# Folding the query and key weights of a cross-attention into one matrix, at the start of a one-core perceiver block

## The chip, the core and the metric

The kernel runs on one core of one Trainium2 chip. A time is the device time of one execution in microseconds (us). The engines are PE (TensorE, matrix products), ACT (ScalarE), DVE (VectorE), POOL (GpSimd) and SP (SyncE, which here only issues DMA transfers). Each engine executes its own list of instructions in order, and engines wait for each other through semaphores.

## The reference

x has 512 tokens of 512 values, ctx has 8192 tokens of 512 values. The block is a cross-attention from x to ctx with a single head, then a linear attention, then a mixture of experts with a convolution, each on a layer norm of x. Only the start of the first step is touched:

```python
qp = layernorm(x) @ Wq.T + bq
kp = ctx @ Wk.T + bk
vp = ctx @ Wv.T + bv
scores = qp @ kp.T * scale          # 512 queries x 8192 keys
x = x + softmax(scores) @ vp @ Wo.T + bo
```

## The kernel before, in words

**Splitting.** Products that need float32 accuracy are made from halves: a matrix a is cut into a high part in the type fp32r (a cast) and a low part (a minus its high part), and a product of two such matrices is three matmuls, high by high, high by low and low by high (`project`, L1162). So each operand costs one cast (mostly on ACT) and one subtraction (on DVE or POOL) before PE can use it.

**Folding of the keys.** ctx is never projected by Wk. The kernel computes qT = Wq times the normalised x, plus bq, and then qk = Wk.T times qT, so that a score is a product of a raw ctx token with a column of qk. This leaves out the dot product of qp with bk, which is the same for all keys of a query. It is needed only where the running maximum is initialised and shifted, and is computed as `key_bias`: DVE multiplies the queries with bk (`qb`, L831), adds the four parts (L852, L855), and PE sums over the partitions by four products with a column of ones (L1281).

**The start, until the first tile of scores.** SP issues the loads in one queue: x and Wq in eight transfers of 256 KB (L337 to L341), the small columns, Wk as one transfer of 1 MB (L343), the first two pairs of transposed ctx tiles, and others. Meanwhile PE multiplies an identity with itself (`warm`, L1179). For each of the four 128-token tiles of x, DVE computes statistics (`ln_stats`), ACT the square root (`std_of`), DVE the scale (`ln_scale`), ACT the normalised tile (`apply_of`), PE its transpose (`transpose_x`), ACT the high half (`high_xT`), DVE the low half (`low_xT`). ACT makes the high halves of Wq and Wk (L550, L570), POOL their low halves (L395, L397). PE computes qT in 96 matmuls of 256 columns (`q_half`), ACT and DVE split it (L589, L833), and PE computes qk in 96 matmuls of 256 columns (L1210 to L1216), which ACT and DVE split again (L602, L840). After that POOL adds bo to x (L410) and, once the last qk product is done, splits Wv (L417, L419).

**The main loop.** In each step s, PE computes one tile of scores for 128 keys (`scores`, L1217, 12 matmuls of 512 columns), ACT copies it to a ring buffer (`keep`), and DVE folds it into a running maximum (`peak`). A tile of scores may start when the peak of the tile two before it is done, since there are two PSUM banks for them. From step 22 on, PE also multiplies exponentials with ctx. Everything on each engine stands in a fixed order that the program writes out; there is no planner.

Of the kernel before, what the change touches and what calls it, by code (L numbers as in the profile page):

```python
# [11 lines left out]
P = 128  # L12
# [32 lines left out]
WARM = 10  # L45
KEEP_WARM = 4
# [19 lines left out]
def perceiver_block(nc, x, ctx_t, ctx_n, wq_t, wk_in, wv_t, wo_t, wqkv_in, wout_in, pieces, cols_in, rows_in, out):  # L66
    with ExitStack() as stack:
# [54 lines left out]
        qT = parts(112, "qT", [P, C, T])  # L122
        qb = at(164, "qb", [P, C, T])
# [22 lines left out]
        block_max, run_max, shift_q, key_bias, biased_max, inv_den = (stat(n) for n in range(6))  # L146
# [61 lines left out]
        wk_loaded = sem("wk_loaded")  # L208
# [7 lines left out]
        wk_high = sem("wk_high")  # L216
        wk_ready = sem("wk_ready")
        wvo_high = sem("wvo_high")
# [22 lines left out]
        q_psum = sem("q_psum")  # L241
        qTh_ready = sem("qTh_ready")
        qTl_ready = sem("qTl_ready")
        qb_step = sem("qb_step")
# [142 lines left out]
        def _(pool):  # L387
# [24 lines left out]
            pool.wait_ge(qk_psum, 2 * C)  # L412
# [94 lines left out]
        Q_BANKS = ((4, 5, 6, 7), (0, 1, 2, 3))  # L507
# [19 lines left out]
        def _(act):  # L527
# [24 lines left out]

            std_of(0)
            apply_of(0)
            high_wq(0)
# [5 lines left out]
            high_wq(1)  # L561
            apply_of(2)
            std_of(3)
            high_wq(2)
            high_xT(2, XT_BANKS)
            apply_of(3)
            high_wq(3)
            high_xT(3, XT_BANKS)
            act.wait_ge(wk_loaded, 16)
            act.copy(wk[0][:], wk_raw[:]).then_inc(wk_high, 1)  # L570
# [14 lines left out]
            def high_q(n):  # L585

                c, h = n % C, n // C * HALF
                act.wait_ge(q_psum, n + 1)
                act.activation(qT[0][:, c, h:h + HALF], bank[:, Q_BANKS[n // C][c], h:h + HALF], ACT.Identity,  # L589
                               bias=col("bq", c)).then_inc(qTh_ready, 1)  # L590

            act.wait_ge(cols_loaded, 16)
            for n in range(C):
                high_q(n)
            for n in range(C):
                high_q(C + n)
                if n < 2:
                    high_ct(n)
            for n in range(2 * C):
                c, h = n % C, n // C * HALF  # L600
                act.wait_ge(qk_psum, n + 1)
                act.copy(qk[0][:, c, h:h + HALF], bank[:, Q_BANKS[n // C][c], h:h + HALF]).then_inc(qkh_ready, 1)  # L602

# [165 lines left out]
        def _(dve):  # L769
# [34 lines left out]

            first_stats(0)
# [10 lines left out]
            low_xT(3, XT_BANKS)  # L816

# [9 lines left out]
            def low_q(n):  # L827
                c, h = n % C, n // C * HALF
                dve.wait_ge(qTh_ready, n + 1)

                dve.tensor_scalar(qb[:, c, h:h + HALF], bank[:, Q_BANKS[n // C][c], h:h + HALF], col("bq", c),  # L831
                                  col("bk", c), ALU.add, ALU.mult).then_inc(qb_step, 1)
                dve.scalar_tensor_tensor(out=qT[1][:, c, h:h + HALF], in0=bank[:, Q_BANKS[n // C][c], h:h + HALF],  # L833
                                         scalar=col("bq", c), in1=qT[0][:, c, h:h + HALF].bitcast(F32), op0=ALU.add,
                                         op1=ALU.subtract).then_inc(qTl_ready, 1)

            def low_qk(n):
                c, h = n % C, n // C * HALF
                dve.wait_ge(qkh_ready, n + 1)
                dve.tensor_tensor(qk[1][:, c, h:h + HALF], bank[:, Q_BANKS[n // C][c], h:h + HALF],  # L840
                                  qk[0][:, c, h:h + HALF].bitcast(F32), ALU.subtract).then_inc(qkl_ready, 1)

            for n in range(C):
                low_q(n)
            for n in range(C):
                low_q(C + n)
                if n < 2:
                    low_ct(n)
            low_qk(0)

            dve.wait_ge(qb_step, 2 * C)
            dve.tensor_tensor(qb[:, 0:2, :], qb[:, 0:2, :], qb[:, 2:4, :], ALU.add).then_inc(qb_step, 1)  # L852
            low_qk(1)
            dve.wait_ge(qb_step, 2 * C + 1)
            dve.tensor_tensor(qb[:, 0, :], qb[:, 0, :], qb[:, 1, :], ALU.add).then_inc(qb_step, 1)  # L855
            for n in range(2, 2 * C):
                low_qk(n)
            dve.wait_ge(keyb_psum, 1)
            dve.tensor_copy(key_bias[:], bank[:, MISC, 0:TT]).then_inc(init_done, 1)
            dve.memset(run_max[:], LOWEST).then_inc(init_done, 1)  # L860
            dve.wait_ge(init_done, 2)
# [18 lines left out]
            def new_shift(n):  # L880

                dve.wait_ge(top_psum, n + 1)
                dve.reduce_max(block_max[:], bank[:, MISC, :].rearrange("p (t k) -> p t k", t=TT),
# [53 lines left out]
            for s in range(TILES + AHEAD - 1):  # L937
# [15 lines left out]
                if s < TILES:  # L953
                    peak(s)

# [199 lines left out]
        def _(pe):  # L1155
# [33 lines left out]
            def q_half(h, e):  # L1189

                pe.wait_ge(xl_ready, 2 * (h + 1))
                pe.wait_ge(wq_ready, e + 1)
                part = slice(h * HALF, (h + 1) * HALF)
                project(Q_BANKS[h][e], [cut(wq, e, c * P, (c + 1) * P) for c in range(C)],
                        [cut(xT, c, part.start, part.stop) for c in range(C)], cols=part).then_inc(q_psum, 1)

            transpose_x(0)
            warm(KEEP_WARM)
            transpose_x(1)
            warm(KEEP_WARM)  # L1200
            q_half(0, 0)
            transpose_x(2)
            q_half(0, 1)
            transpose_x(3)
            q_half(0, 2)
            q_half(0, 3)
            for e in range(C):
# [354 lines left out]
```

## Time and profile before

| what | us |
|---|---|
| median of 3 runs | 556.14 (556.11 to 556.38) |
| the profiled execution's own time | 555.92 |
| its span, first to last instruction | 553.9 |
| PE busy | 542.2 (98%) |
| DVE busy | 350.3 (63%) |
| ACT busy | 257.0 (46%) |
| POOL busy | 201.6 (36%) |

All times of day below are microseconds from the start of the span. A row of the timeline begins with the start and the duration; "x8" says that so many instructions of one kind were merged into the row, with the time from the first start to the last end. A matmul's duration includes the pipeline behind it, so what one costs in a stream is the distance from one start to the next. The square bracket at the end of a row is the idle time before it, with the instruction that ended it.

### The profile page before, as it was taken

What the parts mean: (1) busy time and instruction counts of PE and PEld (TensorE: products, weight loads), DVE (VectorE), ACT (ScalarE), POOL (GpSimd) and SP (SyncE); (2) the same over time, 40 slices, a digit from 0 to 9 for tenths busy, and PEclk for the clock granted to TensorE, in tenths of its full rate; (3) what the DMA queues carried; (4) which work ended last, traced back from release to release, by engine and by line L of the source; (5) the groups of instructions that cost most, each with busy time, mean ns of one, the idle gap of its engine ahead of it and who ended that gap; (6) DMA issues with size and microseconds to landing.
All of it is one profiled execution on the core that took longest, in us unless ns stands there. A gap on an engine that the chain in (4) does not pass through costs nothing. (4 is left out here: it accounts for less than half of the span.)

```text
span 553.9 us, 7074 instructions
## 1 busy us (share of the span) xinstructions
PE 542.2 (98%) x2616; PEld 453.1 (82%) x2616; DVE 350.3 (63%) x574; ACT 257.0 (46%) x420; POOL 201.6 (36%) x125
## 2 busy tenths in 40 slices
PE   8999999999999999999999999979999999999997
PEld 8998888888888888888888887868787889878886
DVE  5845555764667766567766579959736226628757
ACT  6624336754445545445455346546355442561210
POOL 3860512332113251311145133797058709800000
PEclk9999999999999999999999999999999999999999
DMA  8602522425321242232223123132202203300002
GB/s 332 246 14 78 186 83 111 145 84 178 126 77 76 81 148 77 76 141 88 77 76 115 38 115 114 57 134 99 92 0 72 81 1 115 114 1 1 0 2 76
DMA packets 14002, 51.61 MB, mean 93 GB/s; under 512 B 1680, under 2 KB 1680, under 8 KB 13072
## 3 DMA queue, kind: packets, MB, share of 16 engines
q1 hardware_dynamic: 13968, 51.16, 25.7%
q8 instruction: 21, 0.34, 0.3%
q14 instruction: 13, 0.11, 0.1%
HBM read 50.11 MB, written 1.05 MB: 92 GB/s over the span
## 5 line engine op out<-in xcount | busy, mean ns | idle before, releaser
L450 POOL TENSOR_TENSOR cn_l<-raw_n,cn_h 128x1024 fp32r<-128x1024 f32 x32 | 81.3, 2543 | 203.6 <-ACT cn_h L583 203.6
L1241 PE MATMUL bank<-ph,cn_h 128*128 128x512 f32 x256 | 101.5, 396 | 4.7 <-POOL cn_l L450 3.0
L877 DVE TENSOR_TENSOR top<-top,bank 128x512 f32<-128x512 f32 x60 | 41.2, 687 | 101.5 <-ACT ring L607 101.3
L1242 PE MATMUL bank<-pl,cn_h 128*128 128x512 f32 x256 | 100.4, 392 | 0.0
L1243 PE MATMUL bank<-ph,cn_l 128*128 128x512 f32 x256 | 100.3, 392 | 0.0
L1230 PE MATMUL bank<-qk_h,ct_h 128*128 128x512 f32 x256 | 100.0, 391 | 0.0
L1232 PE MATMUL bank<-qk_h,ct_l 128*128 128x512 f32 x256 | 99.7, 389 | 0.0
L1231 PE MATMUL bank<-qk_l,ct_h 128*128 128x512 f32 x256 | 99.6, 389 | 0.0
L613 ACT ACTIVATE ph<-ring 128x512 fp32r<-128x512 f32 x64 | 40.4, 632 | 76.2 <-PE bank L1243 45.2
L607 ACT COPY ring<-bank 128x512 f32<-128x512 f32 x64 | 37.6, 587 | 81.7 <-PE bank L1232 81.7
L1241 PEld LDWEIGHTS bank<-ph,cn_h 128*128 128x128 f32 x256 | 48.4, 189 | 16.0 <-POOL cn_l L450 3.4
L904 DVE TENSOR_TENSOR ring<-ring,shift_b 128x512 f32<-128x512 f32 x64 | 59.4, 928 | 0.0
L1243 PEld LDWEIGHTS bank<-ph,cn_l 128*128 128x128 f32 x256 | 48.5, 189 | 10.4
L1242 PEld LDWEIGHTS bank<-pl,cn_h 128*128 128x128 f32 x256 | 48.5, 189 | 9.8
L1232 PEld LDWEIGHTS bank<-qk_h,ct_l 128*128 128x128 f32 x256 | 48.1, 188 | 10.1
L1230 PEld LDWEIGHTS bank<-qk_h,ct_h 128*128 128x128 f32 x256 | 48.0, 188 | 10.1 <-issue 0.3
L1231 PEld LDWEIGHTS bank<-qk_l,ct_h 128*128 128x128 f32 x256 | 48.1, 188 | 9.8
L912 DVE TENSOR_TENSOR pl<-bank,ph 128x512 fp32r<-128x512 f32 x64 | 43.7, 682 | 7.2 <-ACT bank L618 7.1
L618 ACT ACTIVATE bank<-ring 128x512 f32<-128x512 f32 x64 | 37.6, 588 | 11.1 <-DVE psum_keys L926 10.3
L926 DVE TENSOR_TENSOR psum_keys<-psum_keys,bank 128x512 f32<-128x512 f32 x63 | 42.6, 676 | 0.1
L821 DVE TENSOR_TENSOR ct_l<-raw_t,ct_h 128x1024 fp32r<-128x1024 f32 x32 | 41.0, 1282 | 2.4 <-ACT ct_h L575 2.4
L575 ACT CAST ct_h<-raw_t 128x1024 fp32r<-128x1024 f32 x32 | 33.7, 1052 | 0.0
(214 smaller groups left out, 911.1 us busy)
## 6 DMA issues: line engine op xcount, KB each, us to landing
raw_t<-ctx_t SPq DMA_DIRECT2D x32, 512.0 KB, 4.1
raw_n<-ctx_n SPq DMA_DIRECT2D x32, 512.0 KB, 3.3
piece_raw<-pieces SPq DMA_DIRECT2D x12, 512.0 KB, 3.3
w_raw<-wqkv_in SPq DMA_DIRECT2D x3, 1024.0 KB, 4.9
xs<-x SPq DMA_DIRECT2D x4, 256.0 KB, 3.4
wq_raw<-wq_t SPq DMA_DIRECT2D x4, 256.0 KB, 4.1
wk_raw<-wk_in SPq DMA_DIRECT2D x1, 1024.0 KB, 6.4
wvo_raw<-wv_t SPq DMA_DIRECT2D x1, 1024.0 KB, 11.5
```

The source lines that it names most:

```text
L450: pool.tensor_tensor(cn[p % CNB][1][:], raw_n[p % 2][:], cn[p % CNB][0][:].bitcast(F32), ALU.subtract).then_inc(cnl_ready, 1)
L821: dve.tensor_tensor(ct[p % 2][1][:], raw_t[p % 2][:], ct[p % 2][0][:].bitcast(F32), ALU.subtract).then_inc(ctl_ready, 1)
L877: dve.tensor_tensor(top[n % 2][:], top[n % 2][:], bank[:, S_BANKS[i % 2], :], ALU.max).then_inc(max_done, 1)
L904: dve.tensor_tensor(ring[:, q % RING, :], ring[:, q % RING, :], shift_b[q // SB % 2][:], ALU.subtract).then_inc(sub_done, 1)
L912: dve.tensor_tensor(pl[q % PB][:], bank[:, p_bank(q), :], ph[q % PB][:].bitcast(F32), ALU.subtract).then_inc(pl_ready, 1)
L926: dve.tensor_tensor(psum_keys[:], psum_keys[:], bank[:, p_bank(q), :], ALU.add).then_inc(den_done, 1)
L1230: pe.matmul(bank[:, dst, :], ct[i // 2 % 2][0][:, c, keys], qk[0][:, c, :], start=(c == 0), stop=False)
L1231: pe.matmul(bank[:, dst, :], ct[i // 2 % 2][0][:, c, keys], qk[1][:, c, :], start=False, stop=False)
L1232: ins = pe.matmul(bank[:, dst, :], ct[i // 2 % 2][1][:, c, keys], qk[0][:, c, :], start=False, stop=(c == C - 1))
L1241: pe.matmul(bank[:, c, :], keys[0][:, q % 2, d], ph[q % PB][:], start=first, stop=False)
L1242: pe.matmul(bank[:, c, :], keys[0][:, q % 2, d], pl[q % PB][:], start=False, stop=False)
L1243: return pe.matmul(bank[:, c, :], keys[1][:, q % 2, d], ph[q % PB][:], start=False, stop=final)
```

## The change

Wq and Wk are multiplied with each other first. The new matrix `wqk` = Wq.T Wk (512 by 512) is computed from the weights alone, by 48 matmuls of 512 columns in four steps e, each of which needs one 128-row piece of each weight, and the transposes of the x tiles are placed between them (`transposed_at`). ACT casts it, DVE subtracts (the low half), and PE computes qk = wqk.T times the normalised x in 48 matmuls of 512 columns. The two biases now come in separately: Wk.T bq is added to qk (`qk_bias`), and the bias of a query is the dot product of its normalised x with Wq.T bk, plus the dot product of bq with bk.

```diff
-WARM = 10
-KEEP_WARM = 4
+WARM = 16
@@ SP
-            for t in range(0, TT, 2):
-                for n in range(t, t + 2):
-                    sp.dma_start(xs[:, n, :], x[n]).then_inc(x_loaded[n], 16)
-                for e in range(t, t + 2):
-                    sp.dma_start(wq_raw[:, e, :], wq_t[e]).then_inc(wq_loaded[e], 16)
+            for e in range(C):
+                sp.dma_start(wq_raw[:, e, :], wq_in[e]).then_inc(wq_loaded[e], 16)
+                sp.dma_start(wk_raw[:, e, :], wk_in[e]).then_inc(wk_loaded[e], 16)
+                sp.dma_start(xs[:, e, :], x[e]).then_inc(x_loaded[e], 16)
             sp.dma_start(cols[:], cols_in).then_inc(cols_loaded, 16)
-            sp.dma_start(wk_raw[:], wk_in).then_inc(wk_loaded, 16)
@@ POOL
-            for e in range(C):
-                pool.wait_ge(wq_high, e + 1)
-                pool.tensor_tensor(wq[1][:, e, :], wq_raw[:, e, :], wq[0][:, e, :].bitcast(F32), ALU.subtract).then_inc(wq_ready, 1)
-            pool.wait_ge(wk_high, 1)
-            pool.tensor_tensor(wk[1][:], wk_raw[:], wk[0][:].bitcast(F32), ALU.subtract).then_inc(wk_ready, 1)
+            pool.memset(ones[:], 1.0).then_inc(ones_ready, 1)
+            for e in range(1, C):
+                pool.wait_ge(wk_loaded[e], 16)
+                pool.tensor_copy(wk[0][:, e, :], wk_raw[:, e, :]).then_inc(wk_high, 1)
+                pool.wait_ge(wk_high, e)
+                pool.tensor_tensor(wk[1][:, e, :], wk_raw[:, e, :], wk[0][:, e, :].bitcast(F32), ALU.subtract).then_inc(wk_ready, 1)
...
-            pool.wait_ge(qk_psum, 2 * C)
+            pool.wait_ge(wqk_psum, C)
@@ ACT
+            high_wq(0)
+            act.wait_ge(wk_loaded[0], 16)
+            act.copy(wk[0][:, 0, :], wk_raw[:, 0, :]).then_inc(wk0_high, 1)
             std_of(0)
+            high_wq(1)
             apply_of(0)
             std_of(1)
+            high_wq(2)
             apply_of(1)
             high_xT(0, XT_BANKS)
             std_of(2)
+            high_wq(3)
+            apply_of(2)
             high_xT(1, XT_BANKS)
             std_of(3)
+            apply_of(3)
             high_xT(2, XT_BANKS)
             high_xT(3, XT_BANKS)
+            for c in range(C):
+                act.wait_ge(wqk_psum, c + 1)
+                act.copy(wqk[0][:, c, :], bank[:, WQK_BANKS[c], :]).then_inc(wqkh_ready, 1)
+            for n in range(2):
+                high_ct(n)
+            act.wait_ge(qk_bias_ready, 1)
+            act.wait_ge(bk_step, C)
+            for c in range(C):
+                act.wait_ge(qk_psum, c + 1)
+                act.activation(qk[0][:, c, :], bank[:, QK_BANKS[c], :], ACT.Identity, bias=qk_bias[:, c:c + 1]).then_inc(qkh_ready, 1)
@@ DVE
+            def low_wq(e):
+                dve.wait_ge(wq_high, e + 1)
+                dve.tensor_tensor(wq[1][:, e, :], wq_raw[:, e, :], wq[0][:, e, :].bitcast(F32), ALU.subtract).then_inc(wq_ready, 1)
+            low_wq(0)
+            dve.tensor_tensor(wk[1][:, 0, :], wk_raw[:, 0, :], wk[0][:, 0, :].bitcast(F32), ALU.subtract).then_inc(wk0_ready, 1)
             first_stats(0)
             ln_scale(0)
+            low_wq(1)
             first_stats(1)
             ln_scale(1)
+            low_wq(2)
             first_stats(2)
             low_xT(0, XT_BANKS)
             ln_scale(2)
+            low_wq(3)
             low_xT(1, XT_BANKS)
             first_stats(3)
             ln_scale(3)
             low_xT(2, XT_BANKS)
             low_xT(3, XT_BANKS)
+            for c in range(C):
+                dve.tensor_tensor(wqk[1][:, c, :], bank[:, WQK_BANKS[c], :], wqk[0][:, c, :].bitcast(F32),
+                                  ALU.subtract).then_inc(wqkl_ready, 1)
-            for n in range(C):
-                low_q(n)
-            for n in range(C):
-                low_q(C + n)
-                if n < 2:
-                    low_ct(n)
-            low_qk(0)
...
+            def weigh_rows(dst, raw, loaded, name, step):
+                for e in range(C):
+                    dve.wait_ge(loaded[e], 16)
+                    if e == 0:
+                        ins = dve.tensor_scalar(dst[:], raw[:, e, :], col(name, e), None, ALU.mult)
+                    else:
+                        dve.wait_ge(step, e)
+                        ins = dve.scalar_tensor_tensor(out=dst[:], in0=raw[:, e, :], scalar=col(name, e), in1=dst[:],
+                                                       op0=ALU.mult, op1=ALU.add)
+                    ins.then_inc(step, 1)
+            weigh_rows(bq_wk, wk_raw, wk_loaded, "bq", bq_step)
+            weigh_rows(bk_wq, wq_raw, wq_loaded, "bk", bk_step)
+            dve.tensor_tensor(b_prod[:], cols[:, a:a + C], cols[:, b:b + C], ALU.mult).then_inc(dot_step, 1)
+            dve.wait_ge(dot_step, 1)
+            dve.reduce_sum(b_dot[:, 0:1], b_prod[:], AX.X).then_inc(dot_step, 1)
+            dve.memset(run_max[:], LOWEST).then_inc(run_cleared, 1)
+            for n in range(2):
+                low_ct(n)
+            dve.wait_ge(qk_bias_psum, 1)
+            dve.tensor_copy(qk_bias[:], bank[:, MISC, 0:C]).then_inc(qk_bias_ready, 1)
+            for c in range(C):
+                dve.wait_ge(qkh_ready, c + 1)
+                dve.scalar_tensor_tensor(out=qk[1][:, c, :], in0=bank[:, QK_BANKS[c], :], scalar=qk_bias[:, c:c + 1],
+                                         in1=qk[0][:, c, :].bitcast(F32), op0=ALU.add, op1=ALU.subtract).then_inc(qkl_ready, 1)
+            def key_term(t):
+                dve.tensor_tensor(key_terms[:, t, :], xn[:, t, :], bank[:, U_BANK, :], ALU.mult).then_inc(key_step, 1)
+                dve.wait_ge(key_step, 2 * t + 1)
+                dve.reduce_sum(key_bias[:, t:t + 1], key_terms[:, t, :], AX.X).then_inc(key_step, 1)
...
                 if s < TILES:
                     peak(s)
+                if 2 <= s < 2 + TT:
+                    key_term(s - 2)
@@ PE
+            transposed_at = {(1, 1): 0, (2, 0): 1, (2, 3): 2, (3, 1): 3}
+            for e in range(C):
+                pe.wait_ge(wq_ready, e + 1)
+                if e == 0:
+                    pe.wait_ge(wk0_ready, 1)
+                else:
+                    pe.wait_ge(wk_ready, e)
+                for c in range(C):
+                    fold_part(e, c)
+                    if (e, c) in transposed_at:
+                        transpose_x(transposed_at[e, c])
+            pe.wait_ge(xl_ready, TT)
+            for e in range(C):
+                pe.wait_ge(wqkl_ready, e + 1)
+                if e == C - 1:
+                    pe.wait_ge(bq_step, C)
+                    for c in range(C):
+                        ins = pe.matmul(bank[:, MISC, c:c + 1], bq_wk[:, c * P:(c + 1) * P], ones[:], start=True, stop=True)
+                    ins.then_inc(qk_bias_psum, 1)
+                for c in range(C):
+                    ins = project(QK_BANKS[c], [cut(wqk, e, c * P, (c + 1) * P)], [cut(xT, e, 0, T)], starts=(e == 0),
+                                  stops=(e == C - 1))
@@ PE, after the first tile of scores
-                    for n in range(TT):
-                        ins = pe.matmul(bank[:, MISC, n:n + 1], qb[:, 0, n * P:(n + 1) * P], ones[:], start=True, stop=True)
+                    pe.matmul(bank[:, U_BANK, :], ones[:].to_broadcast([P, P]), bk_wq[:], start=True, stop=True)
+                    pe.matmul(bank[:, MISC, C:C + 1], ones[:].to_broadcast([P, P]), b_dot[:, 0:1], start=True, stop=True)
```

In the diff, `low_wq(e)` makes the low half of one piece of Wq, and `fold_part(e, c)` is a `project` of 3 matmuls of 512 columns. The tiles `qk` lie where `wq_raw` and `wk_raw` lie, so that ACT's first write of `qk` waits for both chains of `weigh_rows`. `scores(0)` waits for the first piece of the low half of qk, as before.

## Rows read from the trace of the kernel before

**Rows 1.** The page, busy time of each engine.
```profile
PE 542.2 (98%) x2616; PEld 453.1 (82%) x2616; DVE 350.3 (63%) x574; ACT 257.0 (46%) x420; POOL 201.6 (36%) x125
```

**Rows 2.** Timeline of PE, from its first product to the second tile of scores.
```profile
1.52 4.64 PE L1181 MATMUL bank<-ident 128*128 128x128 f32 x20 [1.52 <-POOL ident L390]
...
7.00 1.09 PE L1181 MATMUL bank<-ident 128*128 128x128 f32 x8
...
10.12 0.39 PE L1169 MATMUL bank<-xT_h,wq_h 128*128 128x256 f32 x1 [0.56 <-DVE xT_l L797]
...
22.89 0.28 PE L1169 MATMUL bank<-qT_h,wk_h 128*128 128x256 f32 x1
...
34.41 0.40 PE L1230 MATMUL bank<-qk_h,ct_h 128*128 128x512 f32 x1
...
37.16 0.95 PE L1281 MATMUL bank<-ones,qb 128*128 128x1 f32 x8
37.97 0.49 PE L1230 MATMUL bank<-qk_h,ct_h 128*128 128x512 f32 x1
```

**Rows 3.** The loads of Wq (issue line, then landing) and of Wk.
```profile
L341 SPq DMA_DIRECT2D wq_raw<-wq_t x4: 424/432/432, 1.6 to 4.0; - x4
...
DMA to landing us min/median/max: 3.6/4.1/4.6
...
wk_raw<-wk_in SPq DMA_DIRECT2D x1, 1024.0 KB, 6.4
```

**Rows 4.** Timeline of ACT and of DVE over the first x tile.
```profile
5.22 0.81 ACT L545 ACTIVATE xn<-xs,shift,rstd 128x512 f32<-128x512 f32 x1 [0.48 <-DVE shift L790]
5.95 0.60 ACT L550 CAST wq_h<-wq_raw 128x512 fp32r<-128x512 f32 x1
...
3.41 0.69 DVE L781 BATCH_NORM_STATS2 stats<-xs 128x6 f32<-128x512 f32 x1 [3.41 <-DMA xs<-x]
...
4.98 0.21 DVE L790 TENSOR_SCALAR shift<-mv,rstd 128x1 f32<-128x1 f32 x1
...
8.45 0.69 DVE L797 TENSOR_TENSOR xT_l<-bank,xT_h 128x512 fp32r<-128x512 f32 x1 [0.35 <-ACT xT_h L538]
```

**Rows 5.** Groups by line: the first ns min/median/max, the others busy us, mean ns.
```profile
L821 DVE TENSOR_TENSOR ct_l<-raw_t,ct_h x32: 1210/1218/2343, 21.4 to 305.6; 128x1024 fp32r<-128x1024 f32 x32
...
L1137 DVE SCALAR_TENSOR_TENSOR conv<-xf,cols,conv 128x512 f32<-128x512 f32 x12 | 9.0, 752 | 0.4
L667 ACT ACTIVATE vT_h<-bank,cols 128x512 fp32r<-128x512 f32 x4 | 2.7, 689 | 3.4 <-PE bank L1169 3.4
L1135 DVE TENSOR_SCALAR conv<-xf,cols 128x512 f32<-128x512 f32 x4 | 2.2, 542 | 0.0
```

**Rows 6.** Timeline of POOL: the additions of bo, and a cast of Wv.
```profile
23.02 7.04 POOL L410 TENSOR_TENSOR xs<-xs,rows 128x512 f32<-128x512 f32 x4
34.64 1.04 POOL L417 CAST wv_h<-wvo_raw 128x1024 fp32r<-128x1024 f32 x1 [4.58 <-PE bank L1169]
```

**Rows 7.** Timeline of DVE beside POOL, at 29 us and at 354 us.
```profile
29.15 1.45 DVE L855 TENSOR_TENSOR qb<-qb 128x512 f32<-128x512 f32 x1
...
354.04 1.70 DVE L904 TENSOR_TENSOR ring<-ring,shift_b 128x512 f32<-128x512 f32 x1
...
352.33 2.86 POOL L445 TENSOR_TENSOR w_k_l<-w_raw,w_k_h 128x1024 fp32r<-128x1024 f32 x1
355.14 2.86 POOL L450 TENSOR_TENSOR cn_l<-raw_n,cn_h 128x1024 fp32r<-128x1024 f32 x1
```

**Rows 8.** PE after an idle time, then a window; 0.57 is its granted clock.
```profile
370.80 0.50 PE L1241 MATMUL bank<-ph,cn_h 128*128 128x512 f32 x1 [2.98 <-POOL cn_l L450]
...
373.56 0.63 PE L1241 MATMUL bank<-ph,cn_h 128*128 128x512 f32 x1
373.98 0.63 PE L1242 MATMUL bank<-pl,cn_h 128*128 128x512 f32 x1
...
372.00:374.00 2.00, 2.00 (x7) 1.55 (x7) 0.00 (x0) 1.06 (x2) 1.09 (x1) 0.57 0.71 289
```

More of the change, by code:

```diff
@@ L63, with perceiver_block @@
 NROWS = 3 * D + E
-def perceiver_block(nc, x, ctx_t, ctx_n, wq_t, wk_in, wv_t, wo_t, wqkv_in, wout_in, pieces, cols_in, rows_in, out):
+def perceiver_block(nc, x, ctx_t, ctx_n, wq_in, wk_in, wv_t, wo_t, wqkv_in, wout_in, pieces, cols_in, rows_in, out):
     with ExitStack() as stack:
@@ L121, in perceiver_block @@
         wk_raw = at(152, "wk_raw", [P, C, D])
-        qT = parts(112, "qT", [P, C, T])
-        qb = at(164, "qb", [P, C, T])
+        wqk = parts(112, "wqk", [P, C, D])
+        bk_wq = at(164, "bk_wq", [P, D])
+        bq_wk = at(166, "bq_wk", [P, D])
+        key_terms = at(100, "key_terms", [P, TT, D])
         wvo_raw = at(176, "wvo_raw", [P, C, D])
@@ L144, in stat @@
             return small[:, n * TT:(n + width) * TT]
-        block_max, run_max, shift_q, key_bias, biased_max, inv_den = (stat(n) for n in range(6))
+        block_max, run_max, shift_q, key_bias, biased_max, inv_den, b_prod, b_dot, qk_bias = (stat(n) for n in range(9))
         kvmask = at(172.5, "kvmask", [P, VW])
@@ L207, in perceiver_block @@
         wq_loaded = [sem(f"wq_loaded{e}") for e in range(C)]
-        wk_loaded = sem("wk_loaded")
+        wk_loaded = [sem(f"wk_loaded{e}") for e in range(C)]
         wv_loaded = sem("wv_loaded")
@@ L240, in perceiver_block @@
         xf_ready = sem("xf_ready")
[L241 to L244, printed above, removed]
+        wqk_psum = sem("wqk_psum")
+        wqkh_ready = sem("wqkh_ready")
+        wqkl_ready = sem("wqkl_ready")
+        bq_step = sem("bq_step")
+        bk_step = sem("bk_step")
+        dot_step = sem("dot_step")
+        qk_bias_psum = sem("qk_bias_psum")
+        qk_bias_ready = sem("qk_bias_ready")
+        key_step = sem("key_step")
+        run_cleared = sem("run_cleared")
         wr_high = sem("wr_high")
@@ L825, in _ @@
             dve.wait_ge(cols_loaded, 16)
[L827 to L835, printed above, removed]
@@ L849, in _ @@
-            low_qk(0)
[L851 to L859, printed above, removed]
@@ new lines, in key_term @@
+            def key_term(t):
+                dve.wait_ge(keyb_psum, 1)
+                dve.tensor_tensor(key_terms[:, t, :], xn[:, t, :], bank[:, U_BANK, :], ALU.mult).then_inc(key_step, 1)
+                dve.wait_ge(key_step, 2 * t + 1)
+                dve.reduce_sum(key_bias[:, t:t + 1], key_terms[:, t, :], AX.X).then_inc(key_step, 1)
+                if t == TT - 1:
+                    dve.wait_ge(key_step, 2 * TT)
+                    dve.tensor_tensor(key_bias[:], key_bias[:], bank[:, MISC, C:C + 1].to_broadcast([P, TT]),
+                                      ALU.add).then_inc(init_done, 1)
@@ L882, in new_shift @@
                 dve.wait_ge(top_psum, n + 1)
+                if n == 0:
+                    dve.wait_ge(run_cleared, 1)
+                    dve.wait_ge(init_done, 1)
                 dve.reduce_max(block_max[:], bank[:, MISC, :].rearrange("p (t k) -> p t k", t=TT),
@@ L1187, in transpose_x @@
                 transpose_tile(xn, t, XT_BANKS[t]).then_inc(xnT_psum, 1)
-            def q_half(h, e):
-                pe.wait_ge(xl_ready, 2 * (h + 1))
-                pe.wait_ge(wq_ready, e + 1)
[L1193 to L1206, printed above, removed]
-            for e in range(C):
-                q_half(1, e)
-            pe.wait_ge(wk_ready, 1)
-            for h in range(2):
-                pe.wait_ge(qTl_ready, (h + 1) * C)
-                part = slice(h * HALF, (h + 1) * HALF)
+            def fold_part(e, c):
+                d = slice(c * P, (c + 1) * P)
+                ins = project(WQK_BANKS[c], [cut(wq, e, d.start, d.stop)], [cut(wk, e, 0, D)], starts=(e == 0),
+                              stops=(e == C - 1))
+                if e == C - 1:
+                    ins.then_inc(wqk_psum, 1)
@@ L1214, in _ @@
+            for e in range(C):
+                pe.wait_ge(wqkl_ready, e + 1)
+                if e == C - 1:
+                    pe.wait_ge(bq_step, C)
+                    pe.wait_ge(ones_ready, 1)
+                    for c in range(C):
+                        ins = pe.matmul(bank[:, MISC, c:c + 1], bq_wk[:, c * P:(c + 1) * P], ones[:], start=True, stop=True)
+                    ins.then_inc(qk_bias_psum, 1)
                 for c in range(C):
-                    project(Q_BANKS[h][c], [cut(wk, e, c * P, (c + 1) * P) for e in range(C)],
-                            [cut(qT, e, part.start, part.stop) for e in range(C)], cols=part).then_inc(qk_psum, 1)
+                    ins = project(QK_BANKS[c], [cut(wqk, e, c * P, (c + 1) * P)], [cut(xT, e, 0, T)], starts=(e == 0),
+                                  stops=(e == C - 1))
+                    if e == C - 1:
+                        ins.then_inc(qk_psum, 1)
```

58 lines of the change are left out of this document (18 added, 40 removed).

## The prediction, made before the changed kernel had run

> **What bounds the kernel now.** I read the busy times first: PE is busy for 98% of the span [rows 1], so over nearly all of it only PE's work counts. The timeline of PE at the start comes second [rows 2]: the first product with Wq starts at 10.12, the first tile of scores at 34.41, and between them stand 192 matmuls of 256 columns. The 96 of the second product run from 22.89 to 34.41 without a gap, 0.120 us from start to start. The 12 matmuls of 512 columns of a tile of scores go from 34.41 to 37.16, 0.229 us each. After the start nothing of the change touches PE's stream but one small product, so the question is at what time the first tile of scores begins. The third view was the timelines of ACT, DVE and POOL over the first 40 us [rows 4 to 7], because a chain through those three feeds PE there, and the profile's 98% says nothing of how near to it they come.
>
> **PE's own work.** Removed: 192 x 0.120 = 23.0 us. Added: 96 x 0.229 = 22.0. That is a gain of 1.0. The four products with a column of ones (8 instructions, 37.16 to 37.97, 0.81 [rows 2]) now stand inside the second product, as `qk_bias`, and cost 0.8 there. After the first tile of scores come instead one unsplit 128x512 product and one of a single column. A 128-column instruction of that kind takes 1.09/8, about 0.11 with its tail taken off [rows 2], so 512 columns take 2 x 0.44, and the column 0.2: 1.1 for 0.8, a loss of 0.3 (bounds 0 and 1.0).
>
> The Trainium skill has a rule that disputes the gain: TensorE: Matmul & The Clock Gate, section "Back-to-back issue gap", puts an isolated gap at N/2.4 + 2.5 ns. By it an estimate of the saving is 192 x 0.109 less 96 x 0.216, some 0.2 us and not 1.0; the rows' 0.120 and 0.229 differ from it, and they decide.
>
> **Where the first product starts.** Eight loads of 256 KB land from 3.41 (the first, which DVE waited for [rows 4]) to 4.0 + 4.6 = 8.6 [rows 3], 0.74 apart; Wk's megabyte lands at 11.4, the same rate. In the new order that gives Wq's first piece 3.4, Wk's 4.1, x 4.9, and so on to the last x at 11.4. ACT casts (0.60), DVE subtracts (0.69): piece 0 of both is ready at 5.5. But PE first does 16 warm products, 32 instructions. The 20 of before took 4.64 from 1.52, 0.21 each, and from 7.00 on they took half of that: TensorE went from 1.2 to 2.4 GHz at 7.0, after products since 1.52 [rows 2]. So 26 run at the slow rate and 6 at 0.11: the first product starts at 7.7 (5.5 and 8.3 are the bounds; it matters little, as the next paragraph shows).
>
> **The chain through the x tiles.** ACT's `high_xT(0)` now stands ahead of the work on tile 2, and the transpose of tile 0 stands behind 18 matmuls: 7.7 + 18 x 0.229 + 4 x 0.11 = 12.3. Then cast 0.6, `low_xT(0)` 0.7, `ln_scale(2)` 0.4, `apply_of(2)` 0.8 [rows 4]: 14.8. `high_xT(1)`, `low_xT(1)`: 16.1. Statistics to shift of tile 3 take 1.78 (3.41 to 5.19), `apply_of(3)` 0.8: 18.7. PE is ready to transpose tile 3 then as well. Casts of tiles 2 and 3: 20.0, last low half 20.8. ACT casts wqk from 20.0, DVE subtracts its four pieces at 0.6 apart: 21.4 to 23.2. PE has finished wqk at about 20.7, idles 0.8, and starts the second product at 21.5. Without a further wait it ends at 21.5 + 48 x 0.229 + 0.8 = 33.3, 1.1 before the 34.41 of now. PE's 0.8 of idle takes back most of what the products save.
>
> **DVE's queue behind it, which decides.** From 23.2 DVE has, in order: eight operations of `weigh_rows`, three small ones, `low_ct` twice, and only then the copy of `qk_bias`, for which ACT waits before it may write qk, and through it `scores(0)`. Prices: `tensor_scalar` 0.54, `scalar_tensor_tensor` 0.75, in a chain on one tile 0.79 each; `low_ct` 1.22 [rows 5], a small one 0.2, as the shift [rows 4]. Alone that is 2 x (0.55 + 3 x 0.79) + 0.5 + 2.4 = 8.7: the copy ends at 31.8, ACT's 0.69 and DVE's 0.75 give 33.4, and PE would hardly wait.
>
> But POOL works at the same time. Its four additions of bo wait for the last x tile and run from 18.8 to 24.0 (1.3 each alone, 7.04 together beside DVE [rows 6]); its split of Wv, formerly released by the last product at 34.6, is now released at 20.7 and follows at once. The rows show what this does. DVE's addition at 29.15, both inputs in SBUF, took 1.45 for the usual 0.7: it ended 0.55 after POOL's addition did at 30.06 [rows 6, 7]. At 354 it is a pattern: DVE's L904 issued at 354.04, ended at 355.74, 0.55 after POOL's subtraction at 355.19; POOL's next, issued at 355.14, ended 2.26 after DVE's [rows 7]. The two run one after the other, each a whole instruction, turn by turn. With these steps (DVE ends 0.62 after POOL, being 0.07 longer; POOL's subtraction 2.26 after DVE, its cast of 1.04 some 0.9 after):
> bq1 24.6, cast 25.5, bq2 26.1, subtraction 28.4, bq3 29.0, cast 29.9, bk0 29.6, bk1 30.5, subtraction 32.8, bk2 33.4, bk3 34.2; the small ones 34.6, `low_ct` to 37.0, copy 37.1, ACT 37.8, DVE 38.6, PE 38.7.
> This takes the two `tensor_scalar` as free of the collision, as no row shows one; if they take part too, the same steps end at 39.7 and the first chain ends at 30.2, so that the last quarter of the second product also waits. I take the middle, 39.2: 4.8 after the 34.41 of now.
>
> That a `scalar_tensor_tensor` collides is not in my rows, only that a `tensor_tensor` with two inputs in SBUF does. On this the Trainium skill, SBUF — State Buffer, section "Who interferes with whom", says that any DVE instruction with two SBUF inputs contends with a GpSimd one that reads SBUF, and that the second to issue blocks for the whole instruction; the rows agree for the additions. It also names `tensor_scalar` among those that can take the shared ports, which by the steps above would be 39.7, and 0.5 more than my sum.
>
> **The clock.** PE then idles for about 5.5 us, from 33.3 on. In the trace of now PE idled for 2.98 before 370.80 and soon after ran 512-column matmuls 0.42 apart at a granted 0.57, the 1.2 GHz level for the most part [rows 8]; eight of them, some 3.4 us of PE, cost 8 x (0.42 - 0.229) = 1.5. At the start the slow rate lasted 5.5 us [rows 2], which would cost 2.7. I take 2.0.
>
> **What stays hidden.** `key_term` adds 0.7 for the product and 0.7 for the sum (the statistics' 0.69 is the nearest row [rows 4]) in four steps. A step has 2.75 of PE; DVE's own work in two is 2 x 0.6 + 1.15, so four steps hold 10.5 of 11. A tile of scores needs the peak of two tiles before, so DVE may be over a microsecond late. Nothing, at worst 2.8. The smaller warm-up groups and the POOL work on Wk lie beside other work: POOL's piece takes 0.55 + 1.3, ready 2 to 3 us before PE comes to it. The missing `init_done` wait of `high_cn(0)` ends nothing late.
>
> **Sum.** 4.8 + 2.0 + 0.3 = 7.1. The profiled execution took 555.92, with 553.9 of span and 2.0 around it; it becomes 563.0. The median of the runs is 0.2 above it: 563.2.
>
> **Rivals.**
> *The queue fits.* POOL and DVE don't collide on these operations, or POOL's turns fall beside ACT's. For it: DVE's work alone ends at 31.8, and all PSUM-fed DVE operations of the trace keep their time beside POOL. Against: rows 7. PE starts scores at 33.3 to 33.4: -1.0 + 0.3, and up to 1 more if the loads or the clock come early, some 554.9 (553.9 to 556.0). This is the other side; it decides if the copy of `qk_bias` ends before 33.0.
> *Only plain `tensor_tensor` collides.* The chains run freely to 28.9, the product of the biases waits for POOL's second subtraction (to 30.9), `low_ct` follows, copy 33.8, PE 35.4: 1.0 + 0.3 slower with an idle time of 2 that leaves the clock, 557.4.
> *key_term isn't hidden.* Its whole 2.8 stalls scores on top of the forecast: 566.0. Against: the slack above.
>
> **Chances.** The forecast 0.58 (its own range 560.7 to 565.0: half a microsecond from the `tensor_scalar`, 0.7 from the clock, 1 from the x chain), the queue fits 0.24, only `tensor_tensor` 0.10, key_term 0.08. What this kernel's measurement can tell from no change is 0.2%, 1.1 us, so the bound of faster is 555.0. Of the first rival 0.16 lies below it and 0.08 above. With the others: faster 0.17, same 0.10, slower 0.73. The range for 8 in 10 must reach down into the first rival: 554.8 to 565.3.
>
> **What would show it.** Right: DVE's `scalar_tensor_tensor` of `weigh_rows` well over 0.75, most of all 2 to 3 beside POOL's subtractions; ACT's qk activation released by DVE's `qk_bias`; PE idle by 4 to 6 before L1230's successor, then 0.43 spacing. The product of 96 matmuls at 0.229 shows the gain of 1.0. Wrong: all eight at 0.55 to 0.8, POOL's Wv split later, or the second product itself starting after 23.

## The result, and the profile after

| | before | after |
|---|---|---|
| median of the runs, us | 556.12 (555.79 to 556.38) | 562.87 (562.49 to 564.09) |
| ratio, 95% interval | 1 | 1.0125 (1.0108 to 1.0143) |
| profiled execution, us | 555.92 | 562.95 |
| its span, us | 553.9 | 561.2 |
| first tile of scores starts | 34.41 | 39.34 |
| mean granted clock of TensorE | 0.996 | 0.991 |

The change makes the kernel 6.8 us slower; 563.2 was predicted. The busy times say almost nothing of it. PE, with 1.8 us more than in [rows 1], now has 96 instructions fewer, and DVE has 11 us more:

```profile
PE 544.0 (97%) x2520; PEld 449.2 (80%) x2520; DVE 361.6 (64%) x580; ACT 255.5 (46%) x413; POOL 197.3 (35%) x126
```

The timeline of PE, against [rows 2], shows all of it (start us, duration us, engine, line, operation, count, and in brackets the idle time before and what ended it):

```profile
1.52 6.26 PE L1206 MATMUL bank<-ident 128*128 128x128 f32 x32 [1.52 <-POOL ident L397]
7.54 0.48 PE L1194 MATMUL bank<-wk_h,wq_h 128*128 128x512 f32 x1
...
21.55 0.47 PE L1194 MATMUL bank<-xT_h,wqk_h 128*128 128x512 f32 x1 [0.70 <-DVE wqk_l L831]
...
30.02 1.02 PE L1241 MATMUL bank<-ones,bq_wk 128*128 128x1 f32 x8
30.90 0.48 PE L1194 MATMUL bank<-xT_h,wqk_h 128*128 128x512 f32 x1
...
33.52 0.39 PE L1194 MATMUL bank<-xT_h,wqk_l 128*128 128x512 f32 x1
39.34 0.77 PE L1262 MATMUL bank<-qk_h,ct_h 128*128 128x512 f32 x1 [5.43 <-DVE qk_l L869]
39.91 0.63 PE L1263 MATMUL bank<-qk_l,ct_h 128*128 128x512 f32 x1
...
44.41 1.02 PE L1312 MATMUL bank<-bk_wq,ones 128*128 128x512 f32 x2
45.26 0.28 PE L1313 MATMUL bank<-small,ones 128*128 128x1 f32 x2
45.40 0.48 PE L1262 MATMUL bank<-qk_h,ct_h 128*128 128x512 f32 x1
```

Three differences against [rows 2] are to be read here. The scores start at 39.34 for 34.41: 4.93 later. Their first tile lasts from 39.34 to 44.41, 5.07 for 2.75: 2.32 more. What stands behind it lasts from 44.41 to 45.40, 0.99 for 0.81: 0.18 more. Together that is 7.43, and the spans differ by 7.3, so all that comes after the start of the second tile of scores takes back only 0.1.

The windows of the same trace (window, its length, busy us and count of PE, PEld, DVE, ACT and POOL, granted clock, DMA share, GB/s) give the second difference its reason. The granted clock falls while PE is idle (1.00 between 34 and 36, 0.84 between 36 and 38), then stands at 0.50, the 1.2 GHz level, until close to 44:

```profile
36.00:38.00 2.00, 0.00 (x0) 0.00 (x0) 1.62 (x3) 0.34 (x1) 0.00 (x0) 0.84 0.23 63
38.00:40.00 2.00, 0.66 (x2) 0.59 (x3) 1.55 (x3) 2.00 (x4) 0.00 (x0) 0.50 0.91 272
...
44.00:46.00 2.00, 2.00 (x9) 1.30 (x9) 0.69 (x1) 0.59 (x1) 0.00 (x0) 0.96 0.00 0
```

What PE waits for is the end of DVE's queue, which is seen in DVE's timeline:

```profile
23.11 1.11 DVE L848 TENSOR_SCALAR bq_wk<-wk_raw,cols 128x512 f32<-128x512 f32 x1
24.33 5.58 DVE L851 SCALAR_TENSOR_TENSOR bq_wk<-wk_raw,cols,bq_wk 128x512 f32<-128x512 f32 x3
29.84 2.60 DVE L848 TENSOR_SCALAR bk_wq<-wq_raw,cols 128x512 f32<-128x512 f32 x1
32.54 2.47 DVE L851 SCALAR_TENSOR_TENSOR bk_wq<-wq_raw,cols,bk_wq 128x512 f32<-128x512 f32 x3
...
37.47 0.15 DVE L865 COPY small<-bank 128x4 f32<-128x4 f32 x1
38.45 2.73 DVE L869 SCALAR_TENSOR_TENSOR qk_l<-bank,small,qk_h 128x512 fp32r<-128x512 f32 x4 [0.83 <-ACT qk_h L604]
```

The two groups of L851 are the same operation three times, 5.58 us against 2.47. One line's instructions, with their ns (least, median, most), show that they are not uniformly slow:

```profile
L851 DVE SCALAR_TENSOR_TENSOR bq_wk<-wk_raw,cols,bq_wk x3: 1337/1342/2696, 24.3 to 28.6; 128x512 f32<-128x512 f32 x3
L851 DVE SCALAR_TENSOR_TENSOR bk_wq<-wq_raw,cols,bk_wq x3: 751/753/753, 32.5 to 34.3; 128x512 f32<-128x512 f32 x3
```

The last three, at 0.75, start just after POOL has ended its fourth instruction, at 32.16. POOL's timeline of that stretch:

```profile
18.90 5.05 POOL L417 TENSOR_TENSOR xs<-xs,rows 128x512 f32<-128x512 f32 x4 [3.88 <-ACT xn L554]
23.89 1.24 POOL L424 CAST wv_h<-wvo_raw 128x1024 fp32r<-128x1024 f32 x1
25.21 2.71 POOL L426 TENSOR_TENSOR wv_l<-wvo_raw,wv_h 128x1024 fp32r<-128x1024 f32 x1
27.87 1.50 POOL L424 CAST wv_h<-wvo_raw 128x1024 fp32r<-128x1024 f32 x1
29.45 2.71 POOL L426 TENSOR_TENSOR wv_l<-wvo_raw,wv_h 128x1024 fp32r<-128x1024 f32 x1
```

Lay the two beside each other. DVE's three `scalar_tensor_tensor` of `bq` end at 25.67, 28.47 and 29.91, its `bk` 0 at 32.44; POOL's end at 25.13, 27.92, 29.37 and 32.16. Each of DVE's ends 0.54 or 0.55 (the `tensor_scalar` 0.28) after one of POOL's. This looks like turns, each a whole instruction; the experiments test it. And ACT's qk activation was released by DVE's copy:

```profile
37.66 2.42 ACT L604 ACTIVATE qk_h<-bank,small 128x512 fp32r<-128x512 f32 x4 [13.73 <-DVE small L865]
```

`key_term`, the last part, is hidden. Its product (0.68) and sum (0.69) stand in the timeline of DVE four times from 52.41 on, and ACT's copies of the tiles of scores stay 2.72 apart beside them.

### The profile page after: what moved, and what is told of

It reads as the page before. It is cut to its first block and busy times, and to the rows that moved or that the text cites. A ratio compares the mean times of both kernels' runs of the same rounds, so it can differ in the third digit from the quotient of the medians.

```text
span 561.2 us, 6888 instructions
## 1 busy us (share of the span) xinstructions
PE 544.0 (97%) x2520; PEld 449.2 (80%) x2520; DVE 361.6 (64%) x580; ACT 255.5 (46%) x413; POOL 197.3 (35%) x126
## 5 line engine op out<-in xcount | busy, mean ns | idle before, releaser
L837 DVE TENSOR_TENSOR ct_l<-raw_t,ct_h 128x1024 fp32r<-128x1024 f32 x32 | 39.7, 1243 | 1.8 <-ACT ct_h L588 1.8
```

## The experiments

The theory: DVE's queue ahead of the copy of `qk_bias` is late because each of its operations with two inputs in SBUF takes turns with one of POOL's, and the idle time that this makes on PE costs the clock as well. The rivals: DVE's queue is simply too long, or its operations chained on one tile are slow by themselves; or DVE and POOL share bandwidth, each slowed evenly, and take no turns; or the second product, the loads or `key_term` are late. The first four kernels ran beside the kernel before at 556.03 (555.63 to 556.82), the other four beside it at 555.97 (555.73 to 557.04).

**1. `e1_late_split`: POOL's split of Wv waits for the last product, as before the change.**

```diff
-            pool.wait_ge(wqk_psum, C)
+            pool.wait_ge(qk_psum, C)
```

> POOL's split of Wv waits for the last product of qk again instead of the last product of wqk; all else as changed. Turn-taking theory (DVE and POOL instructions that read SBUF twice exclude each other, a whole instruction at a time): only the additions of bo, until 24.0, stand against DVE's chains. bq chain ends at 26.7, bk chain at 29.6, the copy of qk_bias at 32.5, scores begin at 34.2 (39.34 with the change), PE idles by under 1 us and keeps its clock: 555.8 us, range 555.2 to 556.8. Rival, the chained DVE operations are slow by themselves (in-place, one waiting for the other): no change, 562.9. Rival, POOL and DVE share bandwidth evenly: the operations fall from 1.85 to 0.75 too, so this run does not part it from the first.

Measured: 555.73 (554.84 to 556.48), ratio 0.9992 (0.9983 to 1.0002). One wait on another engine gives all of the loss back. What is left of the fold is 0.3 us, which is not clear of the noise. DVE's timeline, then POOL's, then PE's:

```profile
24.33 2.46 DVE L851 SCALAR_TENSOR_TENSOR bq_wk<-wk_raw,cols,bq_wk 128x512 f32<-128x512 f32 x3
26.71 0.48 DVE L848 TENSOR_SCALAR bk_wq<-wq_raw,cols 128x512 f32<-128x512 f32 x1
...
32.22 0.15 DVE L865 COPY small<-bank 128x4 f32<-128x4 f32 x1
```

```profile
33.73 1.04 POOL L424 CAST wv_h<-wvo_raw 128x1024 fp32r<-128x1024 f32 x1 [9.79 <-PE bank L1194]
34.85 2.40 POOL L426 TENSOR_TENSOR wv_l<-wvo_raw,wv_h 128x1024 fp32r<-128x1024 f32 x1
```

```profile
34.09 0.47 PE L1262 MATMUL bank<-qk_h,ct_h 128*128 128x512 f32 x1 [0.43 <-DVE qk_l L869]
```

The same queue with the same instructions is 5.25 us earlier at the copy, and the scores start 5.25 earlier. So the queue is not too long by itself, its operations are not slow by themselves (L851 takes 2.46 for three in both groups), and the second product, the loads and `key_term` are not the cause. Even sharing of bandwidth would give the same result here; the third and fourth kernels part it from the turns. A `tensor_scalar` alone takes 0.48; beside POOL's subtraction it took 2.60. POOL's subtraction at 34.85 runs for its first microsecond beside DVE's operations that read one input from PSUM (until 35.93), and takes the usual 2.4.

**2. `e2_keep_busy`: PE multiplies the identity with itself during the idle time; DVE and POOL unchanged.**

```diff
+            for n in range(24):
+                pe.matmul(bank[:, U_BANK, 0:P], ident[:], ident[:], start=True, stop=True)
             def scores(i):
```

> The changed kernel with 24 extra products of the identity (48 instructions, 5.3 us at 0.11) on PE between the last qk product and the first tile of scores, in a bank that nothing else uses then. Theory that the idle time costs twice, as waiting and as a lower clock behind it: scores still begin at 39.3 to 39.5, but their matmuls stand 0.23 apart and not 0.43, 2.3 us less: 560.6 us (560.2 to 561.0). Rival, the clock falls whatever PE does there or the small products don't hold it: 562.9.

Measured: 560.83 (560.44 to 561.14), ratio 1.0083 (1.0068 to 1.0098).

```profile
34.06 5.52 PE L1250 MATMUL bank<-ident 128*128 128x128 f32 x48
39.63 0.47 PE L1265 MATMUL bank<-qk_h,ct_h 128*128 128x512 f32 x1
```

The scores start no earlier, but their first tile is 2.81 long (39.63 to 42.44) and not 5.07, at a granted clock of 1.00. So the clock's share of the loss is 2.0 us by the medians and 2.3 by the traces, and it follows from PE's idle time.

**3. `e3_small_turns`: Wv and Wo split in pieces of 256 columns, the same work in four times as many instructions.**

```diff
-                    pool.tensor_copy(w[0][:, part, :], ...)
-                    pool.tensor_tensor(w[1][:, part, :], ...)
                     ...
+                    for k in range(4):
+                        c, a = 2 * h + k // 2, k % 2 * 256
+                        pool.tensor_copy(w[0][:, c, a:a + 256], ...)
+                        pool.tensor_tensor(w[1][:, c, a:a + 256], ...)
```

> The changed kernel with POOL's split of Wv and Wo cut into pieces of 256 columns, eight casts and eight subtractions per weight in place of two and two. Turn-taking theory: a DVE operation waits for at most one small POOL instruction (0.3 or 0.65), so a scalar_tensor_tensor beside the split takes 1.0 to 1.4 and none over 1.7; but POOL goes on until 37, so low_ct is met as well: copy of qk_bias at 36, scores at 37.9, 561.3 us (560.3 to 562.3). Rival, even sharing of bandwidth: the operations keep their mean of 1.85 and the time stays at 562.9 or above.

Measured: 559.30 (558.78 to 559.76), ratio 1.0056 (1.0041 to 1.0071). The direction was right, the size was missed by 2.0, outside the stated range. DVE's line, two rows of POOL, and PE's first matmul of scores:

```profile
L852 DVE SCALAR_TENSOR_TENSOR bq_wk<-wk_raw,cols,bq_wk x3: 750/751/1037, 23.7 to 25.7; 128x512 f32<-128x512 f32 x3
```

```profile
23.97 1.11 POOL L427 TENSOR_TENSOR wv_l<-wvo_raw,wv_h 128x256 fp32r<-128x256 f32 x1
25.03 0.85 POOL L425 CAST wv_h<-wvo_raw 128x256 fp32r<-128x256 f32 x1
```

```profile
35.70 0.75 PE L1263 MATMUL bank<-qk_h,ct_h 128*128 128x512 f32 x1 [2.63 <-DVE qk_l L870]
```

I had expected every operation of DVE to wait for a turn, 1.0 to 1.4 each; four of the six took 0.75. The ones that did began 0.14 or 0.15 before the end of a cast (25.73 beside the one that ends at 25.88), and so had next to nothing to wait for. Only the middle one of each chain, issued at 24.59 beside a subtraction that ends at 25.08, took 1.04, and ended 0.55 after it. POOL waited as well: its subtraction took 1.11 here and 0.73 later, beside no such operation of DVE. An operation of DVE thus pays what is left of POOL's instruction when its turn comes, and short instructions leave little. Evenly shared bandwidth does not fit operations of 0.75 and 1.04 beside the same work. After 2.63 us of idle the clock fell again (0.50 between 36 and 38), and the first tile of scores took 4.42 (35.70 to 40.12), 1.6 more than in the second kernel.

**4. `e4_big_turns`: the opposite, one cast and one subtraction of 2048 columns.**

```diff
-                for h in range(2):
-                    pool.tensor_copy(w[0][:, part, :], ...)
-                    pool.tensor_tensor(w[1][:, part, :], ...)
                 ...
+                pool.tensor_copy(w[0][:], wvo_raw[:])
+                pool.tensor_tensor(w[1][:], wvo_raw[:], w[0][:].bitcast(F32), ALU.subtract)
```

> The opposite of the small turns: the split of a weight in one cast (2.0 us) and one subtraction (4.65 us) of 2048 columns. Turn-taking theory: one scalar_tensor_tensor of the bq chain takes some 2.5 and one 5.2 us, the others after them 0.75, since POOL is done by then. The bq chain ends at 32.7 instead of 29.9, so PE's last quarter of qk waits nearly 3 us; the copy of qk_bias at 38.5, scores at 40.2: 563.3 us (562.3 to 564.3). Rival, even sharing: all operations slowed alike, to 1.5 to 2, none at 5, and the time as with the change, 562.9.

Measured: 563.14 (562.61 to 563.84), ratio 1.0129 (1.0112 to 1.0146). DVE's line, POOL's timeline and PE's:

```profile
L848 DVE SCALAR_TENSOR_TENSOR bq_wk<-wk_raw,cols,bq_wk x3: 750/2191/4887, 23.8 to 31.1; 128x512 f32<-128x512 f32 x3
```

```profile
23.31 2.11 POOL L422 CAST wv_h<-wvo_raw 128x2048 fp32r<-128x2048 f32 x1
25.50 4.90 POOL L424 TENSOR_TENSOR wv_l<-wvo_raw,wv_h 128x2048 fp32r<-128x2048 f32 x1
```

```profile
31.91 1.04 PE L1238 MATMUL bank<-ones,bq_wk 128*128 128x1 f32 x8 [2.50 <-issue]
...
39.11 0.47 PE L1259 MATMUL bank<-qk_h,ct_h 128*128 128x512 f32 x1 [1.72 <-DVE qk_l L866]
```

One of DVE's operations of 0.75 took 4.89, the length of POOL's subtraction, one took 2.19, and the third 0.75: turns, and no even sharing. Two operations lose 5.6 us where four lost 5.2 in the changed kernel, and the scores start at 39.11. Part of the clock's loss moves: it falls after PE's 2.50 of idle ahead of the biases' product, is paid in the last quarter of the second product (0.43 between matmuls from 33.39 on), and is back before the scores, which 1.72 us of idle do not slow.

The total, however, was expected rightly by luck. The first tile of scores now takes 2.82 and ends at 41.93, 2.5 before the changed kernel's 44.41, yet the spans differ by only 0.3. Some 2.0 are lost again at 75 us, where POOL splits Wo, also in one piece. POOL's row, DVE's and PE's:

```profile
68.61 4.61 POOL L424 TENSOR_TENSOR wo_l<-wvo_raw,wo_h 128x2048 fp32r<-128x2048 f32 x1
```

```profile
69.29 5.00 DVE L834 TENSOR_TENSOR ct_l<-raw_t,ct_h 128x1024 fp32r<-128x1024 f32 x1 [0.27 <-ACT ct_h L585]
```

```profile
75.04 0.47 PE L1259 MATMUL bank<-qk_h,ct_h 128*128 128x512 f32 x1 [1.92 <-DVE top L894]
```

DVE's subtraction, which takes 1.2 alone, is held for 5.00 behind POOL's; the running maximum comes after it in DVE's queue, and PE waits for that. It is the same cause at a second place, and it was not in my expectation.

**5. `e5_in_gaps`: three of the eight operations of `weigh_rows` put where DVE is idle between x tiles, the other five behind wqk, with `bq` and `bk` alternating so that each is ready when the one before it ends; POOL early as in the change.** The question was whether POOL only gets its turn in a gap of DVE's.

```diff
             first_stats(2)
+            dve.wait_ge(cols_loaded, 16)
+            weigh(0, "bq")
             low_xT(0, XT_BANKS)
             ln_scale(2)
             low_wq(3)
+            weigh(0, "bk")
             ...
+            weigh(1, "bq")
             low_xT(2, XT_BANKS)
             ...
-            weigh_rows(bq_wk, wk_raw, wk_loaded, "bq", bq_step)
-            weigh_rows(bk_wq, wq_raw, wq_loaded, "bk", bk_step)
+            weigh(1, "bk")
+            weigh(2, "bq")
+            weigh(2, "bk")
+            weigh(3, "bq")
+            weigh(3, "bk")
```

> POOL as in the changed kernel (Wv split early), but three of the eight operations of the two bias chains stand in idle stretches of DVE before the second product, and the other five follow it with bq and bk in turn, so that no operation waits for the one just before it. If the ports change hands at the end of every instruction for which the other engine waits: the five end at 33.3, copy of qk_bias 36.1, scores 37.8, the clock lost as before, 561.3 us (560.5 to 562). If POOL only got its turns in the small gap in which DVE waited for its own last result: DVE runs through, copy at 30 to 31, scores at 33.5, about 555.2.

Measured: 560.69 (558.89 to 562.08), ratio 1.0079 (1.0056 to 1.0101). The turns change after every instruction, also where DVE's next is ready at once. DVE's timeline, and PE's:

```profile
24.14 1.52 DVE L819 SCALAR_TENSOR_TENSOR bq_wk<-wk_raw,cols,bq_wk 128x512 f32<-128x512 f32 x1
25.58 2.88 DVE L819 SCALAR_TENSOR_TENSOR bk_wq<-wq_raw,cols,bk_wq 128x512 f32<-128x512 f32 x1
```

```profile
37.02 0.47 PE L1281 MATMUL bank<-qk_h,ct_h 128*128 128x512 f32 x1 [3.14 <-DVE qk_l L888]
```

Beside a cast DVE's operation takes 1.52, beside a subtraction 2.88, and each ends 0.55 after POOL's. In this profiled execution, the fastest of its four at 558.89, PE's first tile of scores took 2.82 (37.02 to 39.84) after 3.14 us of idle: no slow stretch. Where the spread of its times, 3.2 us, comes from is open. A clock that fell in the other three could explain part of it (it cost 1.6 to 2.3 in the kernels above), but those three lie 2.1 apart at one and the same mean granted clock, 0.994, and only the fastest has a trace.

**6. `e6_gaps_late`: the fifth with the wait of the first.** DVE's queue is then shorter and free of POOL.

```diff
  (as e5_in_gaps, and)
-            pool.wait_ge(wqk_psum, C)
+            pool.wait_ge(qk_psum, C)
```

> The same order of DVE, and POOL's split of Wv late again. Both theories: bias chains done by 27, low_ct by 30, copy of qk_bias right after its product at 30.8; scores follow the last qk product at 33.5 without a wait (34.09 with the late split alone): 555.1 us (554.6 to 555.6). Rival, the operations put into the gaps delay the x chain by their own length: 555.7 or more.

Measured: 555.13 (554.73 to 555.42), ratio 0.9982 (0.9973 to 0.9991). PE now goes from the second product into the scores without an idle time. They start 0.90 before the 34.41 of the kernel before, and the medians differ by 0.84:

```profile
33.51 0.39 PE L1281 MATMUL bank<-qk_h,ct_h 128*128 128x512 f32 x1
```

**7. `e7_wqk_first`: also aims at PE's 0.7 of idle between the products**, by casting and subtracting the first quarter of wqk ahead of the x tiles 2 and 3.

```diff
  (as e6_gaps_late, and on ACT; on DVE low_wqk likewise)
+            high_wqk(0)
             high_xT(2, XT_BANKS)
             high_xT(3, XT_BANKS)
-            for c in range(C):
+            for c in range(1, C):
                 high_wqk(c)
```

> As the one before, and the first quarter of wqk is cast and subtracted ahead of the transposes of the last two x tiles, on ACT and DVE: PE's idle time between the two products falls from 0.7 to near 0, the second product starts at 20.8 instead of 21.5: 554.4 us (554.0 to 555.0). Rival, the last x tile is then what PE waits for: no change against the one before.

Measured: 554.36 (553.97 to 554.71), ratio 0.9969 (0.9957 to 0.9981). It is faster than both kernels, 8.5 us below the changed one, with the change's products kept. The scores start 0.86 before the sixth's. Of that, 0.36 is the idle time between the products (0.34 left of 0.70, which the last x tile ends, the wait that the rival named), and 0.5 came with the start of this execution, where the clock rose earlier and PE's first product stands at 6.47, not 7.56. How much of the 0.77 between the two medians is the new order is therefore not settled.

```profile
20.68 0.50 PE L1223 MATMUL bank<-xT_h,wqk_h 128*128 128x512 f32 x1 [0.34 <-DVE xT_l L804]
...
32.65 0.40 PE L1291 MATMUL bank<-qk_h,ct_h 128*128 128x512 f32 x1
```

**8. `e8_warm12`: the seventh with four warm products fewer**, since the first wqk product waited for them and not for the loads.

```diff
-WARM = 16
+WARM = 12
```

> As the one before with 12 warm products in place of 16: the first product starts at 6.7 instead of 7.5, its first matmuls at the slower clock; the transpose of tile 0, which holds ACT's queue, comes 0.7 earlier: 553.8 us (553.3 to 554.4). Rival, the weights' second pieces (ready at 9.6) or the loads of x take over: 554.4 as before.

Measured: 555.54 (553.98 to 556.52, eleven times), ratio 0.9984 (0.9974 to 0.9994): 1.2 slower than the seventh where 0.6 faster was expected. In its trace PE's first product is earlier, 6.09 for 6.47, but at 10 us the engines meet in another order. DVE and POOL of the seventh, then of the eighth:

```profile
10.06 0.69 DVE L814 TENSOR_TENSOR wq_l<-wq_raw,wq_h 128x512 fp32r<-128x512 f32 x1
```

```profile
10.06 1.85 POOL L405 TENSOR_TENSOR wk_l<-wk_raw,wk_h 128x512 fp32r<-128x512 f32 x1
```

```profile
10.06 1.83 DVE L814 TENSOR_TENSOR wq_l<-wq_raw,wq_h 128x512 fp32r<-128x512 f32 x1
```

```profile
10.04 1.29 POOL L405 TENSOR_TENSOR wk_l<-wk_raw,wk_h 128x512 fp32r<-128x512 f32 x1
```

Where both issue at 10.06, DVE takes 0.69 and POOL waits; where POOL is 0.02 us ahead, DVE takes 1.83. That 1.1 us runs down the chain of the x tiles: the last transposes, which PE runs at 18.30 in the seventh, come 1.26 later, and so do the scores (33.92 for 32.65):

```profile
19.56 0.65 PE L1213 MATMUL bank<-ident,xn 128*128 128x128 f32 x4 [1.53 <-ACT xn L554]
```

Whether fewer warm products flip this order, or it falls either way by chance, is not settled. The eleven times lie partly at 554 to 555 and mostly at 555.5 to 556.5, which fits a race that goes both ways, but only one of the eleven has a trace.

## Why the prediction was right

- **PE's own work, -1.0.** Right. 36 matmuls of the second product stand between 21.55 and 29.82, 0.230 each, for the 0.229 predicted.
- **The first product and the x tiles.** 7.54 for 7.7; transposes of tile 0 at 11.75 for 12.3; low halves of wqk up to 23.19 for 23.2; second product at 21.55 for 21.5. It ends at 33.75 and not 33.3, mostly since the biases' product takes 1.08 (29.82 to 30.90, a wait for `bq_wk` in it) and not 0.8. That is hidden in the idle time.
- **DVE's queue beside POOL.** The step that decides, and right: the copy ends at 37.62, predicted 37.1 with the `tensor_scalar` free and about 38 with them colliding. The turns fell otherwise than in my list: `bq` 1 met the first cast, so the first subtraction fell on `bq` 2 and the second on the `tensor_scalar` of `bk`. Both `tensor_scalar` took part, the first held by the last addition of bo (1.11 for 0.48), the second for 2.60. That is the later of my two ends, with the first chain at 30.2 (29.91 measured) and the scores at 39.7 (39.34 measured). I had not decided between the ends and took the middle, 39.2; that it came within 0.14 is luck, as the rule of the later end is the true one and its steps were 0.4 too long. (The 31.8 that I gave for the queue alone is 31.9 by its own terms.)
- The Trainium skill, SBUF — State Buffer, section "Who interferes with whom", names both kinds, an instruction with two SBUF inputs and, as one that can contend, `tensor_scalar`; the trace agrees with both (1.34 and 2.70 for 0.75; 2.60 for 0.48).
- **The clock, 2.0.** Right in kind, 2.32 in the trace. I had sized it from eight slow matmuls at 370 us; it was eleven, the first 0.57 from the next and ten 0.43, up to 44.17.
- **The bias product at the end, 0.3.** It was 0.18: the unsplit 512-column product takes 0.85 (44.41 to 45.26), and the single column 0.14, not 0.2.
- **`key_term`, 0.** Right.
- **The sum.** 4.8 + 2.0 + 0.3 = 7.1; measured 4.93 + 2.32 + 0.18 = 7.43. Between the profiled executions there are 7.03, as 0.1 came back after the second tile and the time around the span was 1.75 here and not 2.0; none of my steps spoke of either. The mechanism and the order of its terms were right; that the median was hit within 0.3 is in part luck, since these small misses have opposite signs.
- **The rivals.** The first, that the queue fits, is what the first experiment brings about, by one wait; its premise, that the two engines don't collide on these operations, was false. I put 554.9 on it with the scores at 33.3 to 33.4; it is 555.73 with them at 34.09, as DVE's queue, whose first `tensor_scalar` still meets the last addition of bo (1.09), ends at 32.37 and not at 31.8. Only `tensor_tensor` colliding (557.4) falls by 1.34 and 2.70 in L851; `key_term` falls by its four places in the trace.

## What to carry to other kernels

When a wait of one engine is moved earlier because its data is ready, ask what the others do at that time: here POOL's work on Wv, needed much later, was let loose beside DVE's only critical stretch, and one wait moved back was worth 7 us. Where DVE reads two inputs from SBUF on the critical path, count up to one whole POOL instruction per DVE instruction as long as POOL has a queue; small pieces on POOL cost less, large ones more. In four traces here an idle time of 2.5 to 5.4 us on PE cost its length and then, in three of them, 1.6 to 2.3 us more of halved clock. Fillers save only the second part (2.0 us in the second kernel); a shorter queue, or POOL's work moved out of its way, saves both.

## What had not been expected of the hardware

- The turn changes at the end of each instruction even where DVE's next is ready at once (1.52 and 2.88 in the fifth kernel). I had thought a dense queue on DVE might keep POOL out. On this the Trainium skill, SBUF — State Buffer, "Who interferes with whom", says that whoever issues first has the pair of SBUF ports that the two share for the whole instruction, and the other blocks; the trace agrees, and 0.02 us of issue order decided 1.1 us in the eighth kernel.
- A `tensor_scalar` with one tile as input takes part in it: 2.60 for 0.48.
- The clock fell after 2.63 us of idle (third kernel) and 2.50 (fourth), and in one execution did not after 3.14 (fifth); 1.72 and 1.92 (fourth) did not slow the matmuls behind them. In the fifth's execution the granted clock is recorded as 0.95 from 5 us on, but for a fall near 374 us, while the matmuls are 0.23 apart, as at 1.00 in the others: the spacing of the matmuls is the safer reading.
- Behind the same warm products the first product started between 6.47 (seventh) and 7.85 (second) from one execution to another. PE ran 16 of them between 4 and 6 us in the third kernel and 12 in the changed one, which reads as a clock that rose earlier or later, though the granted clock is recorded as 1.00 in both. I had written that the start of the first product matters little; it reaches the x chain at about three quarters. POOL's additions of bo, which wait for the last x tile, start at 18.32 where that product starts at 6.76 (third), at 18.90 for 7.54 (the changed kernel) and at 19.20 for 7.85 (second).
